# Layer 2 of a four-layer network on one core: B of the state scan broadcast one state ahead, banks shared anew, routing counts in two matmuls

## The chip, the cores and the metric

The kernel runs on one core of a Trainium2 chip. The metric is the device time of one execution in microseconds; lower is better. TensorE is called PE, VectorE DVE, ScalarE ACT, GpSimd POOL, and SyncE, which issues the DMAs, SP.

## The reference

Four layers follow each other, each an attention-like mixer, a gate computed by a feed-forward part, and `x = x + s * silu(ffn(xn))`. The tokens are 4096 rows of 128 features (the input of 16 x 256 tokens). The change touches layer 2 only. Its mixer is a selective state scan, its feed-forward part a choice of 2 of 16 expert banks for each token:

```
def step(h, inp):                       # 16 states n, 256 channels d
    dt_t, B_t, C_t, u_t = inp
    dA = jnp.exp(dt_t[..., None] * A)
    h = h * dA + (dt_t * u_t)[..., None] * B_t[:, None, :]
    y = jnp.einsum('bdn,bn->bd', h, C_t)
    return (h, y)
...
logits = jnp.einsum('bsd,de->bse', tensor, Wr) + br
probs = jax.nn.softmax(logits, axis=-1)
topv, topi = jax.lax.top_k(probs, NUM_SELECTED)          # 2 of 16
h = jax.nn.relu(jnp.einsum('bsd,edh->bseh', tensor, W1) + b1)
y = jnp.einsum('bseh,ehm->bsem', h, W2) + b2
```

## The kernel before

The stages run one after the other, each a block in which every engine has its own program, and semaphores order them. Two stages matter here.

**Routing** (`layer2_route`). The 4096 tokens go by in 8 chunks of 512 (TT = 4 groups of 128). One loop iteration i finishes layer 1's gate for chunk i (`gate_times`, `gate_finish`), normalises it (`ln_tensor` on PE, `ln_scalar` on ACT, `ln_vector` on DVE), and routes chunk i-1: PE makes the logits and turns the rows, DVE picks two banks of 16 with one-hot masks OA and OB (`select`), PE counts with triangular and all-one matrices how many tokens before each one chose the same bank (`counts`), DVE adds the running offset `r.base` and writes the places (`place`), and POOL scatters the rows with 8 indirect DMAs. DVE's order in an iteration is: copy of Y, product, `select(i-1)`, `gate_finish`, `place(i-1)`, `ln_vector`. PE's is: turn, logits, `ln_tensor`, `counts(i-1)`.

**Scan and experts** (`layer2_mix`). There are 8 chunks k of 512 tokens and 16 states n; g = 16k + n numbers the states. For each state the engines do this:

- PE broadcasts the rows B and C of the state over the partitions (`spread_states`, L1079 and L1081; two matmuls of 32 rows each, on different rows of the array), into banks 0 and 1. It waits first for DVE's drive and ACT's copy of the state before.
- ACT computes the decay DA (L1196, two exponentials) and copies C to CN (L1203).
- DVE multiplies DB = DU x B out of the bank (L1302, the drive) and runs the scan over 1024 columns (L1308), which needs the decay.
- POOL multiplies the state with C: CA for the near half (L1355), CB for the far half (L1362) and its sum YA (L1364). PE adds CA up in bank 5 (`add_near`, L1089, one state later).

Between the states lie two other lines of work. The head of chunk k+1 (`head(k + 1, n)`: norm, input projection, convolution, silus, dt, on steps 0 to 14) is spread over the steps of chunk k. And in steps 3 to 12 one tile of 128 routed rows a step goes through its expert, 10 tiles a chunk, 80 in all: PE turns the rows (`tile_rows`, L1105), ACT copies them to XT (L1209), PE multiplies with the first weights (`tile_hidden`, L1110), ACT applies relu (L1214, buffer H), PE multiplies with the second weights and adds the bias (`tile_out`, L1118 and L1119), ACT copies the result to YO (L1221) and SP stores it. At the end of a chunk DVE gates the sum (L1314 to L1320), PE projects it (`project`, L1096) and DVE adds the input (L1326).

PE's queue is in order, and its order in a step is written out by hand: B and C; `tile_rows(j)`; `tile_out(j-1)`; `tile_hidden(j)`; `project` in step 1; `add_near` of the state before; the head's matmuls. The expert's weights (578 KB a tile) and its rows (64 KB) have two buffers, and SP's program for them is:

```
for j in range(TILES):
    if j >= 2:
        sp.wait_ge(s.out_ready, j - 1)
    load_tile(j)
    if j >= 2:
        store_tile(j - 2)
```

`out_ready` is raised by the last matmul of `tile_out`, so that the load of tile j follows `tile_out(j-2)`, and `tile_rows(j)` waits for the load.

## Time and profile before

| | |
|---|---|
| three runs | 4656.27, 4648.75, 4588.19 us; median 4648.75 |
| profiled execution | 4658.04 us, span 4656.4 us |
| busy | PE 3423.9 us (74%), DVE 2642.8 (57%), ACT 1828.2 (39%), POOL 1538.3 (33%) |
| granted clock of PE, mean | 0.793 of 2.4 GHz |
| DMA | 111.46 MB in the whole, 63 GB/s in the scan stage |

Busy shares are means over stages with different limits; PE's busy time has modelled ends and is no measure of a full PE. The granted clock is at one of two levels at each moment, 1.0 (2.4 GHz) or 0.5 (1.2 GHz); a figure between is a mean over a stretch. The profile's "idle before" of an instruction tells what released its engine.

### The profile page before, as it was taken

To read this page: it belongs to the slowest core of one execution; us is meant where nothing else is said; L and a number is where in the kernel's file an instruction comes from. 1 tells how busy PE (TensorE), PEld (TensorE's weight loads), DVE (VectorE), ACT (ScalarE), POOL (GpSimd) and SP (SyncE) were. 2 spreads that over 40 slices of the span, in tenths; PEclk is the share of its full clock that TensorE was granted. 3 is DMA by queue.
4 is the path that set the end of the run, shared out by engine and by line. 5 is a ranking of instruction groups with operands and counts; after the bars stand their busy time and mean duration, and the time that the engine had idled before them with its cause. 6 is when DMAs were issued, how large, how long until landed. Compare 5 with 4: busy or idle time off the path is not lost. (4 is left out here: it accounts for less than half of the span.)

```text
span 4656.4 us, 50785 instructions
## 1 busy us (share of the span) xinstructions
PE 3423.9 (74%) x17802; PEld 1842.6 (40%) x17802; DVE 2642.8 (57%) x3696; ACT 1828.2 (39%) x3692; POOL 1538.3 (33%) x1231
## 2 busy tenths in 40 slices
PE   5888888883538788788757677676776857778587
PEld 3444444441424344344323334333343334343343
DVE  3444444442547777777655566555665656556565
ACT  3333333331214444444424434344343434434344
POOL 0000000003316665656644253332533424334242
PEclk8888888885557777777768879688797988959789
DMA  1000000002212222222100000000000000000000
GB/s 80 7 7 7 7 7 7 7 5 74 72 42 63 67 67 67 67 67 59 59 16 5 8 1 5 8 5 8 1 5 8 5 8 1 8 6 5 8 1 8
DMA packets 70704, 111.46 MB, mean 24 GB/s; under 512 B 8640, under 2 KB 46016, under 8 KB 69952
## 3 DMA queue, kind: packets, MB, share of 16 engines
q1 hardware_dynamic: 65088, 97.47, 6.5%
q0 software_dynamic: 5376, 11.02, 0.9%
q8 instruction: 123, 2.02, 0.2%
q14 instruction: 117, 0.96, 0.1%
HBM read 81.71 MB, written 26.74 MB: 23 GB/s over the span
## 5 line engine op out<-in xcount | busy, mean ns | idle before, releaser
L369 ACT ACTIVATE l_PT<-PB 128x512 f32<-128x512 f32 x512 | 277.9, 594 | 539.1 <-PE PB L280 539.1
L280 PE MATMUL PB<-l_QM,l_KP 32*128 32x256 f32 x2048 | 375.2, 497 | 131.6 <-DVE l_QM L418 75.9
L407 DVE TENSOR_REDUCE keep_MXP<-PB 128x4 f32<-128x1024 f32 x256 | 301.5, 1220 | 106.8 <-PE PB L253 106.8
L280 PEld LDWEIGHTS PB<-l_QM,l_KP 32*128 32x128 f32 x2048 | 241.3, 243 | 256.4 <-ACT l_PT L369 99.9
L1308 DVE TENSOR_TENSOR_SCAN l_ST<-l_DA,l_DB 128x1024 f32<-128x1024 f32 x128 | 313.7, 2451 | 42.0 <-ACT l_DA L1196 32.8
L1355 POOL TENSOR_TENSOR l_CA<-l_ST,l_CN 128x512 f32<-128x512 f32 x128 | 182.6, 1426 | 397.6 <-DVE l_ST L1308 346.0
L703 POOL MEMSET l_KV<- 128x4 f32 x8 | 0.8, 105 | 918.5 <-POOLq L109 918.5
L1515 POOL TENSOR_TENSOR l_PT<-l_PT,l_PEN 128x512 f32<-128x512 f32 x168 | 212.5, 1284 | 184.5 <-ACT l_PT L369 184.5
L1089 PE MATMUL PB<-l_CA,consts 128*128 128x512 f32 x256 | 199.2, 872 | 71.4 <-POOL l_CA L1355 71.4
L1779 POOL TENSOR_TENSOR l3f_SQ<-l3f_RW 128x512 f32<-128x512 f32 x128 | 146.8, 1147 | 302.4 <-ACT l3f_RW L1645 302.4
L1302 DVE TENSOR_TENSOR l_DB<-l_DU,PB 128x1024 f32<-128x1024 f32 x128 | 155.4, 1214 | 154.1 <-PE PB L1079 153.4
L1583 PE MATMUL PB<-l3f_QK 64*64 64x128 f32 x2048 | 159.3, 301 | 80.5 <-DVE l3f_QK L1719 80.5
L1788 POOL TENSOR_TENSOR l3f_PP<-l3f_PP,l3f_RS 128x512 f32<-128x512 f32 x128 | 133.1, 1040 | 251.2 <-DVE l3f_RS L1737 251.2
L1079 PE MATMUL PB<-l_BC,consts 32*128 32x512 f32 x256 | 180.9, 792 | 42.7 <-DVE l_DB L1302 22.0
L253 PE MATMUL PB<-l_KP,l_QP 32*128 32x256 f32 x2048 | 198.0, 514 | 15.6 <-issue 15.6
L1362 POOL TENSOR_TENSOR l_CB<-l_ST,l_CN 128x512 f32<-128x512 f32 x120 | 208.8, 1740 | 0.0
L1670 ACT ACTIVATE l3f_PP<-PB,l3f_MN 128x128 f32<-128x128 f32 x512 | 146.4, 368 | 157.6 <-DVE l3f_MN L1731 157.6
L294 PE MATMUL PB<-l_PT,keep_VT 128*32 128x256 f32 x2048 | 170.6, 490 | 35.2 <-POOL l_PT L1515 19.2
L418 DVE TENSOR_TENSOR l_QM<-l_QP,PB 128x256 f32<-128x256 f32 x128 | 53.9, 421 | 237.0 <-PE PB L262 233.5
L1364 POOL TENSOR_TENSOR l_YA<-l_YA,l_CB 128x512 f32<-128x512 f32 x120 | 184.2, 1535 | 9.4
L1401 POOL TENSOR_SCALAR l_T<-l_AJ,l_GI 128x256 f32<-128x256 f32 x16 | 18.4, 1147 | 504.0 <-DVE l_AJ L1491 504.0
L1081 PE MATMUL PB<-l_BC,consts 32*128 32x512 f32 x256 | 182.1, 797 | 0.0
(416 smaller groups left out, 7934.3 us busy)
## 6 DMA issues: line engine op xcount, KB each, us to landing
l_WB<-in_w2f_dram SPq DMA_DIRECT2D x80, 578.0 KB, 3.4
l_XR<-xs_mid SPq DMA_DIRECT2D x80, 64.0 KB, 3.5
ys_mid<-l_YO SPq DMA_DIRECT2D x80, 64.0 KB, 3.3
w3fs<-in_w3f_dram SPq DMA_DIRECT2D x1, 3125.0 KB, 16.6
keep_XI<-in_x_dram SPq DMA_DIRECT2D x9, 256.0 KB, 3.0
x_mid<-keep_X SPq DMA_DIRECT2D x9, 256.0 KB, 3.0
s_mid<-keep_S SPq DMA_DIRECT2D x9, 256.0 KB, 2.0
keep_SI<-s_mid SPq DMA_DIRECT2D x9, 256.0 KB, 2.6
```

The source lines that it names most:

```text
L253: last = nc.tensor.matmul(PB[:, r, qt * SEQ:(qt + 1) * SEQ], b.QP[rows, a, q0:q0 + 128], b.KP[rows, a, i, sq * SEQ:(sq + 1) * SEQ], start= ...
L280: last = nc.tensor.matmul(PB[:, 4 + u % STBANKS, kt * SEQ:(kt + 1) * SEQ], b.KP[rows, a, i, k0:k0 + 128], b.QM[rows, n % 2, :], start=True ...
L369: nc.scalar.activation(b.PT[:, u % PSLOTS].rearrange("p k q -> p (k q)"), PB[:, 4 + u % STBANKS, :], ACT.Exp).then_inc(s.exp_done, 1)
L407: nc.vector.tensor_reduce(dst[:, 2 * pair:2 * pair + 2, :, 16 + n % 2], PB[:, 2 * pair:2 * pair + 2, :].rearrange("p r (t k) -> p r t k", ...
L1079: nc.tensor.matmul(PB[:, 0, :], c.ident[0:32, n:n + 1].broadcast_to([32, 128]), b.BC[0:32, k % 2, :], start=True, stop=True).then_inc(s.b_ ...
L1081: nc.tensor.matmul(PB[:, 1, :], c.ident[32:64, 32 + n:33 + n].broadcast_to([32, 128]), b.BC[32:64, k % 2, :], start=True, stop=True).then_ ...
L1089: last = nc.tensor.matmul(PB[:, 5, :], c.ident, b.CA[:, g % 2, :], start=n == 0, stop=n == NS - 1)
L1308: nc.vector.tensor_tensor_scan(b.ST[:, g % 2].rearrange("p k t -> p (k t)"), b.DA[:, g % 2].rearrange("p k t -> p (k t)"), b.DB[:, g % 2]. ...
L1355: nc.gpsimd.tensor_tensor(b.CA[:, g % 2, :], b.ST[:, g % 2, 0, :], b.CN[:, g % 2, :], ALU.mult).then_inc(s.near_ready, 1)
L1362: nc.gpsimd.tensor_tensor(b.CB[:], b.ST[:, g % 2, 1, :], b.CN[:, g % 2, :], ALU.mult).then_inc(s.far_ready, 1)
L1364: last = nc.gpsimd.tensor_tensor(b.YA[:], b.YA[:], b.CB[:], ALU.add)
L1515: nc.gpsimd.tensor_tensor(pt, pt, b.PEN[:, 2 * sq:2 * sq + 2, :], ALU.mult).then_inc(s.weighed_pool, 1)
```

## The change

In the scan stage `spread_states` is split. `spread_drive(g)` broadcasts B into bank g % 2, one PE step ahead of its state, and waits for the drive of state g-2. `spread_output(g)` broadcasts C into bank 2 and waits for the copy of C of state g-1 alone. The turned rows of a tile and the tile's result now share bank 3 (the projection uses it too), and the hidden product moves to bank 4. PE's order in a step becomes: B of the next state, C of this one; `tile_rows(j)`; `project`; `add_near`; `tile_hidden(j)`; `tile_out(j-1)`; head. `tile_rows(j)` now waits for the result copy of tile j-2, `tile_hidden(j)` for the activations of tile j-1, and ACT's activations of tile j for `tile_out(j-1)`. ACT's own order, DVE's, POOL's and SP's stay.

In the routing stage the 14 count matmuls become two over all 64 columns, done ahead of `ln_tensor`; DVE forms the running offsets of the four groups in `r.base`, now five rows, with four chained adds, and `place` comes behind `ln_vector`.

```diff
-                    for t in range(TT):
-                        o = PB[:, 6, t * E2:(t + 1) * E2]
-                        nc.tensor.matmul(o, c.before, b.OC[:, t, :], start=True, stop=t == 0)
-                        for u in range(t):
-                            nc.tensor.matmul(o, c.ones, b.OC[:, u, :], start=False, stop=u == t - 1)
-                    for t in range(TT):
-                        last = nc.tensor.matmul(PB[:, 6, TT * E2:TT * E2 + E2], c.ones, b.OC[:, t, :], start=t == 0, stop=t == TT - 1)
-                    last.then_inc(s.count_ready, 1)
+                    each = b.OC[:].rearrange("p t e -> p (t e)")
+                    nc.tensor.matmul(PB[:, 6, 0:TT * E2], c.before, each, start=True, stop=True)
+                    nc.tensor.matmul(PB[:, 6, TT * E2:2 * TT * E2], c.ones, each, start=True, stop=True).then_inc(s.count_ready, 1)
...
                     if i:
                         logits(i - 1)
+                        counts(i - 1)
                     if i < CHUNKS:
                         pe.wait_ge(s.x_gated, i + 1)
                         ln_tensor(nc, pe, s, c, of(i).X, PB[:, 1:5], i)
-                    if i:
-                        counts(i - 1)
...
-                    link(nc.vector.tensor_tensor(b.WK[:], PB[:, 6, 0:TT * E2].rearrange("p (t e) -> p t e", e=E2),
-                                                 r.base[:].unsqueeze(1).broadcast_to([128, TT, E2]), ALU.add))
-                    nc.vector.tensor_tensor(r.base[:], r.base[:], PB[:, 6, TT * E2:TT * E2 + E2], ALU.add).then_inc(s.count_taken, 1)
+                    for t in range(TT):
+                        link(nc.vector.tensor_tensor(r.base[:, t + 1, :], r.base[:, t, :], PB[:, 6, (TT + t) * E2:(TT + t + 1) * E2], ALU.add))
+                    nc.vector.tensor_tensor(b.WK[:], PB[:, 6, 0:TT * E2].rearrange("p (t e) -> p t e", e=E2), r.base[:, 0:TT, :],
+                                            ALU.add).then_inc(s.count_taken, 1)
+                    dve.wait_ge(s.count_taken, k + 1)
+                    nc.vector.tensor_copy(r.base[:, 0, :], r.base[:, TT, :])
...
-                def spread_states(k, n):
-                    g = NS * k + n
+                def spread_drive(g):
+                    k, n = divmod(g, NS)
                     if n == 0:
                         pe.wait_ge(s.bc_copied, k + 1)
+                    if g >= 2:
+                        pe.wait_ge(s.drive_ready, g - 1)
+                    nc.tensor.matmul(PB[:, g % 2, :], c.ident[0:32, n:n + 1].broadcast_to([32, 128]), b.BC[0:32, k % 2, :],
+                                     start=True, stop=True).then_inc(s.b_ready, 1)
+
+                def spread_output(g):
+                    k, n = divmod(g, NS)
                     if g:
-                        pe.wait_ge(s.drive_ready, g)
                         pe.wait_ge(s.c_copied, g)
...
                 def tile_rows(j):
                     pe.wait_ge(tile_loaded[j % 2], 32 * (j // 2 + 1))
-                    if j:
-                        pe.wait_ge(s.rows_taken, j)
+                    if j >= 2:
+                        pe.wait_ge(s.out_taken, j - 1)
...
                 def tile_hidden(j):
                     pe.wait_ge(s.rows_taken, j + 1)
+                    if j:
+                        pe.wait_ge(s.hid_done, 4 * j)
...
-                        spread_states(k, n)
+                        g = NS * k + n
+                        if g == 0:
+                            spread_drive(0)
+                        if g + 1 < NS * CHUNKS:
+                            spread_drive(g + 1)
+                        spread_output(g)
                         j = SLOTS * k + n - FIRST
                         if FIRST <= n < FIRST + SLOTS:
                             tile_rows(j)
-                        if FIRST < n <= FIRST + SLOTS:
-                            tile_out(j - 1)
-                        if FIRST <= n < FIRST + SLOTS:
-                            tile_hidden(j)
...
                             add_near(k, n - 1)
+                        if FIRST <= n < FIRST + SLOTS:
+                            tile_hidden(j)
+                        if FIRST < n <= FIRST + SLOTS:
+                            tile_out(j - 1)
...
                 def tile_hidden(j):
                     act.wait_ge(s.hid_ready, j + 1)
+                    if j:
+                        act.wait_ge(s.out_ready, j)
```

## Rows read from the trace of the kernel before

**Rows 1.** Windows by stage: busy us (instructions) per engine, TensorE clock, DMA share, GB/s.

```profile
1390.00:2345.00 955.00, 753.66 (x2479) 375.92 (x2480) 681.89 (x442) 447.62 (x976) 582.57 (x376) 0.74 0.21 63
```

**Rows 2.** Windows of chunk 3's tile steps and end steps, and of chunk 4's tile steps.

```profile
1767.10:1844.30 77.20, 68.41 (x250) 38.32 (x251) 51.18 (x36) 38.80 (x92) 42.37 (x30) 0.76 0.31 91
1844.30:1889.90 45.60, 29.61 (x65) 10.26 (x65) 36.38 (x24) 18.82 (x34) 30.99 (x19) 0.70 0.06 17
...
1889.90:1964.10 74.20, 63.86 (x258) 36.65 (x259) 52.21 (x35) 39.02 (x92) 41.58 (x30) 0.84 0.29 94
```

**Rows 3.** Waits in the scan stage: us in total, times, longest.

```profile
DVE l_DB L1302 <- PE PB L1079: 153.4, 54, 8.0
...
PEld PB L1105 <- DMA l_XR<-xs_mid: 82.5, 42, 3.4
...
PE PB L1105 <- DMA l_XR<-xs_mid: 42.6, 29, 2.6
...
DVE l_ST L1308 <- ACT l_DA L1196: 32.8, 23, 2.4
```

**Rows 4.** Timeline of a plain tile step: start us, us, engine, line, operation.

```profile
1787.42 0.33 PE L1105 MATMUL PB<-consts,l_XR 128*128 128x128 f32 x1 [0.66 <-DMA l_XR<-xs_mid]
...
1788.58 0.48 PE L1119 MATMUL PB<-l_WB,consts 1*128 1x128 f32 x2
...
1788.99 1.16 PE L1110 MATMUL PB<-l_XT,l_WB 128*128 128x128 f32 x8
...
1790.34 0.33 SPq L1006 DMA_DIRECT2D l_WB<-in_w2f_dram  x1
...
1790.94 0.69 PE L1079 MATMUL PB<-l_BC,consts 32*128 32x512 f32 x1
...
1794.39 0.33 PE L1105 MATMUL PB<-consts,l_XR 128*128 128x128 f32 x1 [2.32 <-DMA l_XR<-xs_mid]
```

**Rows 5.** Timeline: hidden product and `add_near` at 1.2 GHz.

```profile
1716.48 2.08 PE L1110 MATMUL PB<-l_XT,l_WB 128*128 128x128 f32 x8
...
1718.35 1.92 PE L1089 MATMUL PB<-l_CA,consts 128*128 128x512 f32 x2
```

**Rows 6.** Timeline of chunk 3: state 3's product, states 8 and 10.

```profile
1770.74 1.27 POOL L1355 TENSOR_TENSOR l_CA<-l_ST,l_CN 128x512 f32<-128x512 f32 x1 [2.46 <-DVE l_ST L1308]
...
1806.40 2.08 PE L1110 MATMUL PB<-l_XT,l_WB 128*128 128x128 f32 x8 [1.41 <-ACT l_XT L1209]
...
1823.71 1.31 ACT L1196 ACTIVATE l_DA<-l_DL,keep_aneg 128x510 f32<-128x510 f32 x2
1823.79 1.22 DVE L1302 TENSOR_TENSOR l_DB<-l_DU,PB 128x1024 f32<-128x1024 f32 x1 [8.02 <-PE PB L1079]
...
1825.11 2.29 DVE L1308 TENSOR_TENSOR_SCAN l_ST<-l_DA,l_DB 128x1024 f32<-128x1024 f32 x1
```

**Rows 7.** Timeline of a chunk's end (chunks 2 and 3).

```profile
1746.24 1.26 POOL L1364 TENSOR_TENSOR l_YA<-l_YA,l_CB 128x512 f32<-128x512 f32 x1
...
1747.54 1.74 DVE L1317 SCALAR_TENSOR_TENSOR l_YG<-l_XC,w2s,l_YA 128x512 f32<-128x512 f32 x1 [1.67 <-POOL l_YA L1364]
...
1759.79 1.31 ACT L1196 ACTIVATE l_DA<-l_DL,keep_aneg 128x510 f32<-128x510 f32 x2
...
1761.19 2.29 DVE L1308 TENSOR_TENSOR_SCAN l_ST<-l_DA,l_DB 128x1024 f32<-128x1024 f32 x1 [0.39 <-ACT l_DA L1196]
```

**Rows 8.** Routing: timeline of one iteration; the last line is from the waits.

```profile
1230.09 0.22 DVE L874 TENSOR_TENSOR l2r_LO<-PB,w2s 128x64 f32<-128x64 f32 x1 [0.71 <-PE PB L813]
...
1236.37 2.07 PE L132 MATMUL PB<-l2r_X,consts 128*128 128x256 f32 x4 [5.43 <-DVEq L925]
...
1239.84 0.42 ACT L145 ACTIVATE keep_lnr<-keep_lnr 128x256 f32<-128x256 f32 x1
...
1245.97 0.23 DVE L896 TENSOR_TENSOR l2r_WK<-PB,r_base 128x64 f32<-128x64 f32 x1 [9.71 <-PE PB L831]
...
DVE l2r_WK L896 <- PE PB L831: 71.4, 8, 9.7
```

More of the change, by code:

```diff
@@ L913, in _ @@
                 nc.vector.memset(r.gate[:, :, TT * CHUNKS:], 0.0)
-                link(nc.vector.tensor_copy(r.base[:], c.expert))
+                link(nc.vector.tensor_copy(r.base[:, 0, :], c.expert))
                 for i in range(CHUNKS + 1):
@@ L925, in _ @@
                         dve.sem_inc(s.x_gated, 1)
-                    if i:
-                        place(i - 1)
                     if i < CHUNKS:
@@ L932, in _ @@
                         ln_vector(nc, dve, s, c, of(i).XN, PB[:, 1:5], link, i).then_inc(s.xn_ready, 1)
-                nc.vector.tensor_scalar(tails[:], r.base[:], 0.0, None, ALU.add).then_inc(s.tails_ready, 1)
+                    if i:
+                        place(i - 1)
+                nc.vector.tensor_scalar(tails[:], r.base[:, TT, :], 0.0, None, ALU.add).then_inc(s.tails_ready, 1)
                 full = c.full.unsqueeze(1).broadcast_to([128, E2, TOKENS // 128])
@@ L937, in _ @@
                 ends = b.EN[:].unsqueeze(1).broadcast_to([128, TILES, E2])
-                link(nc.vector.tensor_tensor(b.CT[:], r.base[:], c.expert, ALU.subtract))
+                link(nc.vector.tensor_tensor(b.CT[:], r.base[:, TT, :], c.expert, ALU.subtract))
                 link(nc.vector.tensor_tensor(b.NF[:], b.CT[:].unsqueeze(2).broadcast_to([128, E2, TOKENS // 128]), full, ALU.is_gt))
@@ L1093, in project @@
                     pe.wait_ge(s.y_gated, k + 1)
-                    pe.wait_ge(s.rows_taken, SLOTS * (k + 1))
+                    pe.wait_ge(s.out_taken, SLOTS * (k + 1))
                     for h in range(2):
-                        last = nc.tensor.matmul(PB[:, 2, :], w.out[:, h * 128:(h + 1) * 128], b.YG[:, h, :], start=h == 0, stop=h == 1)
+                        last = nc.tensor.matmul(PB[:, 3, :], w.out[:, h * 128:(h + 1) * 128], b.YG[:, h, :], start=h == 0, stop=h == 1)
                     last.then_inc(s.mamba_ready, 1)
@@ L1100, in tile_rows @@
                     pe.wait_ge(tile_loaded[j % 2], 32 * (j // 2 + 1))
-                    if j:
-                        pe.wait_ge(s.rows_taken, j)
+                    if j >= 2:
+                        pe.wait_ge(s.out_taken, j - 1)
                     if j % SLOTS == 0 and j:
                         pe.wait_ge(s.s_added, j // SLOTS)
-                    nc.tensor.transpose(PB[:, 2, 0:128], b.XR[:, j % 2, :], c.ident).then_inc(s.rows_ready, 1)
+                    nc.tensor.transpose(PB[:, 3, 0:128], b.XR[:, j % 2, :], c.ident).then_inc(s.rows_ready, 1)
                 def tile_hidden(j):
                     pe.wait_ge(s.rows_taken, j + 1)
+                    if j:
+                        pe.wait_ge(s.hid_done, 4 * j)
                     for i in range(4):
-                        last = nc.tensor.matmul(PB[:, 3, i * 128:(i + 1) * 128], b.WB[:, j % 2, i * 128:(i + 1) * 128], b.XT[:], start=True, stop=True)
+                        last = nc.tensor.matmul(PB[:, 4, i * 128:(i + 1) * 128], b.WB[:, j % 2, i * 128:(i + 1) * 128], b.XT[:], start=True, stop=True)
                     last.then_inc(s.hid_ready, 1)
@@ L1833, in network @@
         r2 = record(idx=whole("idx2", 2, tokens // 128 + TT), places=whole("places2", 2, TT), bank=whole("bank2", TILES),
-                    row=whole("row2", TILES), **buffers(nc, ctx, "r2", gate=[2, tokens // 128 + TT], base=[E2])._asdict())
+                    row=whole("row2", TILES), **buffers(nc, ctx, "r2", gate=[2, tokens // 128 + TT], base=[TT + 1, E2])._asdict())
         with ExitStack() as first:
```

22 lines of the change are left out of this document (9 added, 13 removed).

## Prediction

> **What bounds the kernel now.** I read the stage windows first, then the waits of the scan stage, then its timeline step by step. The profiled execution took 4658.04 us for a span of 4656.4, 1.6 us around it. The diff touches two stages: the routing, eight loop iterations between 1120 and 1315 us, and layer 2's scan, 955 us [rows 1]. The scan stage is 8 chunks of 16 states, about 7.4 us a state, and no engine fills it (DVE 682 us, POOL 583, PE 754 with modelled ends). So I asked in which order PE's queue releases the others. A chunk has two parts [rows 2]: the ten steps 3 to 12 with an expert tile (77.2 us here, 74.2 in chunk 4) and the six steps around the chunk's end (45.6 us).
>
> In the tile steps the reader is to see a loop that runs through the DMA queue. SP may load tile j only when `tile_out(j-2)` has ended. In one such step [rows 4] `tile_out` ends at 1788.58 + 0.48 = 1789.06; SP issues the weight load at 1790.34, 1.28 us later, and the transpose of the tile after next starts at 1794.39: 5.33 us for the round trip. Between the two PE does useful work: `tile_hidden` at 1788.99, `add_near`, the B/C pair at 1790.94. Then it still waits. 71 of the 80 transposes waited for a load, 82.5 + 42.6 = 125.1 us in all [rows 3]. Right behind the transpose comes `tile_out(j-1)` (1787.42 to 1789.06, 1.6 us), so a plain cycle now is 5.33 + 1.6 = 6.95 us.
>
> DVE waits 153.4 us for B in 54 places [rows 3], which is what the change is aimed at. But the scan behind it needs ACT's decay too: 32.8 us of waits beside, and in most places both arrive together. At 1823.79 DVE had waited 8.02 us for B, and the scan started at 1825.11, just behind the decay's end at 1823.71 + 1.31 = 1825.02 [rows 6]. An earlier B would have bought nothing.
>
> **The change, part by part.**
>
> *B one state ahead, two banks.* No instruction is added. B(g+1) is issued a PE step earlier and waits for the drive of g-1; C(g) alone waits for the copy of C(g-1). DVE's wait for B goes; next late is the decay. Going through the stage's timeline, I took for each wait the smaller of DVE's idle time and the decay's lead: steps 2, 8, 10, 12 and 13 give nothing, the rest about 3 us a chunk with a head and 20 in the last, 40 of 153.4 us. That is the upper bound. Most lies in tile steps, where the loop below decides, and the six steps at the chunk's end don't move either [rows 7]: POOL works without a gap until its add of 1746.24 lets DVE's 1747.54 start, then gate, `project`, `add_near`, the variance matmul, two ACT operations and the decay (1759.79) give the scan of 1761.19. None of these waits for B. I take 0; bound 0 to -40. C and B ran side by side on two row groups. In the tile steps both waits are long satisfied when PE comes to them and that stays; apart they would cost one more pair (1.1 us), hidden under the load wait. 0.
>
> *The tile order.* PE's old order in a step: B/C, transpose(j), `tile_out(j-1)`, `tile_hidden(j)`, `add_near`, head. New: B/C, transpose(j), `add_near`, `tile_hidden(j)`, `tile_out(j-1)`, head. SP's program is the same, so the load of the tile after next is still tied to the end of `tile_out`. `add_near` and `tile_hidden`, which lay inside the round trip, now lie between transpose and `tile_out`, outside it. Queued behind the wait for the load on PE are all of them, and DVE, ACT and POOL behind those. The B/C pair (1.1 us) and no more is left to fill the 5.33 us in a step without head work: this is where cover is lost. Price: `tile_hidden` to the end of `add_near`, as one sequence, 1788.99 to 1790.94 = 1.95 us at a granted 2.4 GHz [rows 4], and 1716.48 to 1718.35 + 1.92, 3.8 us, at 1.2 GHz [rows 5]. The tile window's granted clock is 0.76 [rows 2], half the time at each level, so 2.85 us. New plain cycle: 6.95 + 1.95 = 8.9 us at full clock.
> - Of the eight cycles of a chunk that depend on a load (tiles 2 to 9), five are plain: 40 x 2.85 = 114 us (78 to 152).
> - Three have other work in the chain. Step 5: the transpose no longer lets `tile_out` go first, and `add_near` then waits for POOL's product of the state just scanned, 1.27 us long [rows 6]: +1.5 us. Steps 8 to 9: ACT's table loads and silus, the decay and two copies come behind the hidden activations, and `tile_hidden` waited 1.41 us for XT already [rows 6]; now `tile_out` (1.6 us) stands behind that too, and `add_near` at most: +1 to +3, I take 2. The step with four head matmuls hides the round trip either way: +0.5. Together 4 x 8 = 32 us (12 to 50).
> - ACT's new wait: H(j) and all behind it on ACT (the head's activations, the next decay) wait for `tile_out(j-1)`. In the last tile step this sits in front of the table loads and the decay on which scan 13 waits; before, `tile_hidden` alone did. One `add_near` more, 1.1 to 2.1 us, 8 times: +14 (8 to 20).
>
> Sum of the scan stage: +160 us; the ends are +85 (full clock, some look-ahead kept) and +225 (half clock).
>
> *Banks.* Transpose and result share bank 3, B/C/tile use 0, 1, 2, 3, 4. The transpose waits for the result copy of tile j-2, which ACT does 0.3 us behind `tile_out(j-2)`, 5 us before the load lands: 0.
>
> *Routing.* One loop iteration is 24 us. DVE finishes the gate, PE starts the norm at 1236.37, and DVE sits 9.71 us until the counts are there, at 1245.97; eight such waits are 71.4 us [rows 8]. PE does the layer norm first and then 14 small matmuls. Now two matmuls are done before the norm, in the time in which DVE gates. What is late next: the norm's reciprocal root, first half at 1239.84 + 0.42 = 1240.26, 4.0 us behind the gate's end instead of 9.7: -5.7. `place` moves behind `ln_vector`, so it covers PE's logits, on which DVE waited 0.7: -0.7. Four chained 16-column adds and a copy for one add: +0.9, estimated at the 0.2 us a link that such small operations stand apart. Net -5.5 us, 7 iterations: -38. At the end POOL's queue holds: the scatters of chunk 6 last 10 us and those of 7 stand behind, so the last iteration gives 1 us at most. Moved past SP's and POOL's queues is only `place`'s release of the scatters, 8 x 1.26 us in an 18 us iteration: covered. I take -37 (-30 to -42).
>
> **Total:** +160 - 37 = +123 us, so 4658 + 123 = 4781 for a profiled run. The median shown is 9 us under that run: 4648.75 + 123 = 4772, written as 4770.
>
> **The clock.** In the window of the plain cycles PE's granted clock is 0.76; in the six steps at the chunk's end, with longer gaps between matmuls, 0.70 [rows 2]. With 8.9 us cycles PE waits over 3 us in each. The Trainium skill ("TensorE: Matmul & The Clock Gate", section "HAM oscillation — how this bites in real kernels") says that a loop which waits for a DMA between short bursts of matmuls falls back to half clock in every round. By the row above the price of half clock in all cycles is 3.8 us instead of 2.85, and the lengthened rows the same way. This is rival 2; the rule alone would give its time.
>
> **Rivals.**
> 1. *The same loop, but the clock stays full in the tile steps* and the three special cycles absorb: +85 - 37 = +48, 4697 us. For: nearly half of the windows are at 2.4 GHz now. Against: the gaps get longer.
> 2. *Half clock throughout the tile steps:* +225 - 37 = +188, 4837 us. For: row and rule above. Against: chunk 4 ran 0.84 at cycles of 6.7 us.
> 3. *Faster: the look-ahead decides, and the longer cycle doesn't bind.* DVE's 40 us are saved and routing gives 37: 4572 us. It needs the load to be there when PE comes to the transpose, that is a round trip under the 1.1 us pair plus the head; from 71 waits of 80 I hold it for unlikely. It decides if PE's wait for the load in a plain step stays under about 2 us.
> 4. *The change doesn't do what it says:* C's wait on the copy of C(g-1) stalls the pair in each step and B is no earlier where it matters. Then the gain in the scan is nil, as in my forecast, and the time is the forecast's.
>
> **How the numbers follow.** Forecast with rival 4: 0.58; rival 1: 0.20; rival 2: 0.12; rival 3: 0.07; something that cancels to about zero: 0.03. Two per cent of 4648.75 is 93 us, about what a measurement of this kernel can tell from no change; the limit above is 4742. Of the forecast's own spread some 0.10 lies under it. So slower 0.60, within 2% 0.33, faster 0.07. The range for 8 in 10: from 4695 (rival 1) to 4845 (rival 2).
>
> **What would show it.** In the changed profile: transposes start about 5.3 us behind the end of `tile_out` of two tiles before, as now, but PE's waits for the load rise from 125 us to 300 or more; tile steps take 9 to 12 us each, none 6.7; the tile part of a chunk is 90 to 97 us, the six other steps 44 to 46. DVE's wait for B is nearly gone, its scan waits for the decay instead, and DVE's busy time is unchanged. Routing: iterations of 18.4 us, the wait for the counts gone, 4 us of wait for the root in its place. The prediction is wrong if the transposes find the load landed, if the end part shrinks by more than 2 us a chunk, or if the granted clock in the tile part moves outside 0.6 to 0.85.

## The result, and the profile after

The changed kernel took 4850.26 us in the median of four runs (4829.98 to 4865.49), the kernel before 4641.16 (four runs, 4588.19 to 4656.27): a ratio of 1.047, with a 95% interval of 1.038 to 1.056. It is slower, as forecast, but at +209 us instead of +123, and its time lies 5 us above the upper end of the range. All medians and ranges here and below hold every execution, while the ratios leave out the few of the kernel before that ran in the chip's slower state. The profiled execution took 4865.49 us for a span of 4863.8, 207.4 more than the span of before.

The windows by stage show where these lie. First those of before, of whose three stages only the middle one stands in [rows 1], there from 1390 to 2345; here the bounds are the issue of the scan's first input (1347) and the end of its last scan (2335), so that the stage is 988 us and not the 955 of the prediction. The columns are those of [rows 1], the granted clock is the third figure from the right.

```profile
0.00:1347.00 1347.00, 964.92 (x5194) 564.88 (x5194) 563.17 (x1144) 419.81 (x795) 111.85 (x123) 0.77 0.07 26
1347.00:2335.00 988.00, 773.95 (x2506) 381.39 (x2506) 695.53 (x460) 463.00 (x993) 576.43 (x375) 0.74 0.21 63
2335.00:4656.00 2321.00, 1685.00 (x10103) 896.38 (x10102) 1384.09 (x2093) 945.34 (x1904) 850.06 (x734) 0.83 0.02 6
```

The same three stages of the changed kernel:

```profile
0.00:1304.00 1304.00, 924.14 (x4994) 525.22 (x5002) 568.78 (x1176) 419.81 (x795) 108.26 (x123) 0.79 0.08 27
1304.00:2478.00 1174.00, 792.79 (x2504) 415.68 (x2504) 680.02 (x460) 457.23 (x993) 576.34 (x374) 0.72 0.17 53
2478.00:4864.00 2386.00, 1735.97 (x10016) 935.87 (x10104) 1382.29 (x2092) 944.50 (x1904) 850.85 (x735) 0.79 0.02 6
```

The scan stage is 186 us longer, with DVE, ACT and POOL no busier than before. The first line holds layers 0 and 1 and the routing, 43 us less. The last line holds layer 3, which the diff doesn't touch: 65 us more, DVE, ACT and POOL busy within 2 us of before, PE at a granted clock of 0.79 instead of 0.83. So the +207 is two effects of the change (+186 and about -39, below) and two things that it did not edit: 65 us in layer 3 and -4 in layers 0 and 1.

**The tile loop** is the prediction's loop. These are chunk 3's tile steps and its end steps, against [rows 2]:

```profile
1791.60:1887.00 95.40, 67.07 (x249) 42.45 (x248) 51.07 (x36) 37.24 (x90) 41.64 (x30) 0.73 0.22 67
1887.00:1936.90 49.90, 34.34 (x69) 11.70 (x68) 35.70 (x25) 19.74 (x34) 31.96 (x19) 0.63 0.10 29
```

The waits of the scan stage (us in total, times, longest), against [rows 3]:

```profile
DVE l_ST L1316 <- issue: 331.4, 46, 12.4
...
PEld PB L1106 <- DMA l_XR<-xs_mid: 272.2, 64, 6.1
PE PB L1106 <- DMA l_XR<-xs_mid: 219.3, 64, 5.3
...
DVE l_ST L1316 <- ACT l_DA L1202: 53.0, 9, 6.4
```

The drive's wait for B has no line any more (153.4 us before). The scan waits in its place. Its wait is put down to "issue", but it is the decay: all 60 scans of the trace that waited began 0.09 to 0.44 us behind the decay's end. The two rows of PE and PEld tell of the same transposes, first of the weight load and then of the matmul of each, so they must not be added. Taken by the matmul rows alone, PE's waits for the load went from 42.6 us in 29 places to 219.3 in 64, and these 64 are all the transposes whose load is tied to the loop.

A plain tile cycle, against [rows 4]. To read it, take the end of `tile_out` (the second line of L1120, 1821.92 + 0.27 = 1822.19), the weight load that SP issues (1823.47), and then the next transpose (L1106, 1827.49), which waits for a load. That load, issued at 1823.47, is the one that this end released.

```profile
1817.21 0.34 PE L1106 MATMUL PB<-consts,l_XR 128*128 128x128 f32 x1 [2.34 <-DMA l_XR<-xs_mid]
1817.38 1.02 PE L1090 MATMUL PB<-l_CA,consts 128*128 128x512 f32 x2
...
1818.24 1.68 PE L1113 MATMUL PB<-l_XT,l_WB 128*128 128x128 f32 x8
1819.71 1.92 PE L1119 MATMUL PB<-l_WB,l_H 128*128 128x128 f32 x8
...
1821.92 0.27 PE L1120 MATMUL PB<-l_WB,consts 1*128 1x128 f32 x1
...
1823.47 0.33 SPq L1003 DMA_DIRECT2D l_WB<-in_w2f_dram  x1
...
1827.49 0.48 PE L1106 MATMUL PB<-consts,l_XR 128*128 128x128 f32 x1 [4.43 <-DMA l_XR<-xs_mid]
1827.76 1.92 PE L1090 MATMUL PB<-l_CA,consts 128*128 128x512 f32 x2
...
1829.46 1.92 PE L1113 MATMUL PB<-l_XT,l_WB 128*128 128x128 f32 x8
...
1831.17 1.52 PE L1119 MATMUL PB<-l_WB,l_H 128*128 128x128 f32 x8
...
1832.84 0.27 PE L1120 MATMUL PB<-l_WB,consts 1*128 1x128 f32 x1
```

The round trip is 1822.19 to 1827.49, 5.30 us, as it was (5.33). What changed is the stretch from the transpose to the end of `tile_out`: 1817.21 to 1822.19 = 4.98 us, and 1827.49 to 1833.11 = 5.6 in the next cycle, where it had been 1.6. In the second of them, behind a wait of 4.43 us, the transpose (0.48 us), `add_near` (1.92) and `tile_hidden` (1.92) run at 1.2 GHz, where full clock gives 0.33, 1.02 and 1.16. Over `tile_out` behind them the granted clock is 0.75 in the mean: part of it runs at 2.4 GHz again.

The step with ACT's silus shows what the scan waits for:

```profile
1834.47 1.28 ACT L1170 ACT_TABLE_LOAD   x1
...
1837.90 1.28 ACT L1174 ACT_TABLE_LOAD   x1
...
1839.19 1.33 ACT L1202 ACTIVATE l_DA<-l_DL,keep_aneg 128x510 f32<-128x510 f32 x2
...
1840.61 2.29 DVE L1316 TENSOR_TENSOR_SCAN l_ST<-l_DA,l_DB 128x1024 f32<-128x1024 f32 x1 [12.37 <-issue]
```

DVE had its drive ready 12.37 us before the scan, and the scan still started at the decay's end, 1839.19 + 1.33 = 1840.52. The table loads before it stood behind the activations of the tile, and these behind `tile_out`.

The chunk's end, against [rows 7]:

```profile
1915.96 1.26 POOL L1372 TENSOR_TENSOR l_YA<-l_YA,l_CB 128x512 f32<-128x512 f32 x1
1917.49 1.49 DVE L1325 SCALAR_TENSOR_TENSOR l_YG<-l_XC,w2s,l_YA 128x512 f32<-128x512 f32 x1
...
1929.58 1.31 ACT L1202 ACTIVATE l_DA<-l_DL,keep_aneg 128x510 f32<-128x510 f32 x2
1930.98 2.29 DVE L1316 TENSOR_TENSOR_SCAN l_ST<-l_DA,l_DB 128x1024 f32<-128x1024 f32 x1 [3.82 <-issue]
```

From POOL's add to the scan it is 15.02 us, before 14.95. The windows from drive to drive make the end part look 4 us longer (49.9 against 45.6), because the drive of state 13 now runs ahead of its scan. Counted from scan to scan (scan 13 of a chunk to scan 2 of the next) the seven chunk ends take 35.5 us in the mean, before 35.8; the other part of these seven chunks, scan 2 to scan 13, takes 107.4 against 84.8.

One routing iteration, against [rows 8]:

```profile
1149.72 0.69 DVE L915 COPY keep_Y<-PB 128x512 f32<-128x512 f32 x1
...
1155.44 0.63 PE L827 MATMUL PB<-l2r_OC,consts 128*128 128x64 f32 x2
...
1161.66 0.43 DVE L153 TENSOR_TENSOR keep_lnt<-keep_lnr 128x256 f32<-128x256 f32 x1 [4.13 <-ACT keep_lnr L145]
...
1168.42 0.69 DVE L915 COPY keep_Y<-PB 128x512 f32<-128x512 f32 x1
```

The iteration takes 18.7 us (24 before), and the wait of 4.1 us for the root stands where 9.7 us for the counts stood. From the first copy of Y to the scan's first input the routing took 225.2 us before (1121.85 to 1347.03) and 186.6 after (1117.45 to 1304.07): -38.6.

### The profile page after: what moved, and what is told of

Same layout as the page of the kernel before. It is cut to its first block and busy times, and to the rows that moved or that the text cites. A ratio compares the mean times of both kernels' runs of the same rounds, so it can differ in the third digit from the quotient of the medians.

```text
span 4863.8 us, 50294 instructions
## 1 busy us (share of the span) xinstructions
PE 3452.9 (71%) x17514; PEld 1876.8 (39%) x17610; DVE 2631.1 (54%) x3728; ACT 1821.5 (37%) x3692; POOL 1535.5 (32%) x1231
## 5 line engine op out<-in xcount | busy, mean ns | idle before, releaser
L1316 DVE TENSOR_TENSOR_SCAN l_ST<-l_DA,l_DB 128x1024 f32<-128x1024 f32 x128 | 305.4, 2386 | 391.0 <-issue 331.4
L280 PE MATMUL PB<-l_QM,l_KP 32*128 32x256 f32 x2048 | 390.2, 514 | 131.6 <-DVE l_QM L418 76.0
L1363 POOL TENSOR_TENSOR l_CA<-l_ST,l_CN 128x512 f32<-128x512 f32 x128 | 197.2, 1541 | 583.6 <-DVE l_ST L1316 581.6
L1090 PE MATMUL PB<-l_CA,consts 128*128 128x512 f32 x256 | 226.2, 982 | 103.3 <-POOL l_CA L1363 103.3
L1591 PE MATMUL PB<-l3f_QK 64*64 64x128 f32 x2048 | 171.1, 317 | 88.0 <-DVE l3f_QK L1727 80.5
L253 PE MATMUL PB<-l_KP,l_QP 32*128 32x256 f32 x2048 | 209.8, 541 | 15.6 <-issue 15.6
L294 PE MATMUL PB<-l_PT,keep_VT 128*32 128x256 f32 x2048 | 182.4, 518 | 34.1 <-POOL l_PT L1523 19.2
L1370 POOL TENSOR_TENSOR l_CB<-l_ST,l_CN 128x512 f32<-128x512 f32 x120 | 192.7, 1606 | 0.0
L1106 PE MATMUL PB<-consts,l_XR 128*128 128x128 f32 x80 | 34.4, 430 | 219.3 <-DMA l_XR<-xs_mid 219.3
L1082 PE MATMUL PB<-l_BC,consts 32*128 32x512 f32 x256 | 175.2, 769 | 19.6 <-ACT l_CN L1209 19.6
L1591 PEld LDWEIGHTS PB<-l3f_QK 64*64 64x64 f32 x2048 | 136.4, 159 | 115.5 <-issue 112.3
```

Of the source, the lines that this page charges most:

```text
L253: last = nc.tensor.matmul(PB[:, r, qt * SEQ:(qt + 1) * SEQ], b.QP[rows, a, q0:q0 + 128], b.KP[rows, a, i, sq * SEQ:(sq + 1) * SEQ], start= ...
L280: last = nc.tensor.matmul(PB[:, 4 + u % STBANKS, kt * SEQ:(kt + 1) * SEQ], b.KP[rows, a, i, k0:k0 + 128], b.QM[rows, n % 2, :], start=True ...
L294: last = nc.tensor.matmul(PB[32 * r:32 * r + 32, 7, 0:SEQ], VT[:, 2 * sq + kt, 8 * a + 2 * r + i, :], b.PT[:, (NR * (2 * j + i) + r) % PSL ...
L1090: last = nc.tensor.matmul(PB[:, 5, :], c.ident, b.CA[:, g % 2, :], start=n == 0, stop=n == NS - 1)
L1316: nc.vector.tensor_tensor_scan(b.ST[:, g % 2].rearrange("p k t -> p (k t)"), b.DA[:, g % 2].rearrange("p k t -> p (k t)"), b.DB[:, g % 2]. ...
L1363: nc.gpsimd.tensor_tensor(b.CA[:, g % 2, :], b.ST[:, g % 2, 0, :], b.CN[:, g % 2, :], ALU.mult).then_inc(s.near_ready, 1)
```

## The experiments

Eleven runs: ten other kernels and the changed one again, in three sets, each set timed in rounds beside the kernel before on one chip; the first set (route_only, old_order, no_lookahead, three_buffers) ran on one chip and the other two on another. The medians of before in the three sets were 4637.17 us (19 runs), 4621.88 (7) and 4637.73 (13). "Scan stage" is from the issue of its first input to the end of its last scan; before it was 988.2 us. That is one trace; route_only, whose scan stage is the same code, gives a second value for the old stage, 959.2. Losses of the stage below are counted from 988.2 and would be 29 us larger from the other.

| kernel | scan stage us | granted clock in it | layer 3 us | clock in it | median us | ratio, 95% interval |
|---|---|---|---|---|---|---|
| before, the profiled execution | 988.2 | 0.738 | 2321.1 | 0.827 | | |
| changed, first trace | 1173.7 | 0.717 | 2386.1 | 0.794 | 4850.26 | 1.047 (1.038 to 1.056) |
| route_only | 959.2 | 0.760 | 2350.4 | 0.809 | 4611.04 | 0.994 (0.990 to 0.998) |
| old_order | 1108.8 | 0.691 | 2341.9 | 0.815 | 4718.54 | 1.017 (1.011 to 1.022) |
| no_lookahead | 1173.9 | 0.717 | 2309.9 | 0.828 | 4809.62 | 1.040 (1.035 to 1.045) |
| three_buffers | 992.4 | 0.751 | 2334.3 | 0.818 | 4638.61 | 1.002 (0.999 to 1.005) |
| after_again | 1173.8 | 0.715 | 2311.2 | 0.828 | 4807.37 | 1.039 (1.033 to 1.045) |
| order_alone | 1176.9 | 0.716 | 2330.2 | 0.818 | 4835.46 | 1.046 (1.039 to 1.052) |
| shared_alone | 1104.5 | 0.701 | 2314.0 | 0.825 | 4769.63 | 1.031 (1.025 to 1.037) |
| best_three | 931.2 | 0.779 | 2304.2 | 0.830 | 4549.95 | 0.985 (0.979 to 0.992) |
| route_outfirst | 941.2 | 0.787 | 2310.9 | 0.829 | 4568.41 | 0.986 (0.977 to 0.994) |
| outfirst_three | 945.2 | 0.773 | 2337.2 | 0.817 | 4589.05 | 0.993 (0.989 to 0.998) |
| near_ahead | 1099.4 | 0.675 | 2329.1 | 0.818 | 4761.57 | 1.026 (1.018 to 1.035) |

For the orders I read off the timeline, for each of the eight steps whose load is tied to the loop, the trip (end of `tile_out(j-2)` to the transpose of tile j) and the stretch (that transpose to the end of `tile_out(j-1)`). The two together are one cycle. A trip near 5.3 us is the load's round trip; a longer one holds work that takes longer than the load. Medians over the chunks, in us:

| step | 5 | 6 | 7 | 8 | 9 | 10 | 11 | 12 | sum |
|---|---|---|---|---|---|---|---|---|---|
| before, trip | 7.17 | 5.37 | 5.26 | 5.65 | 7.13 | 7.54 | 5.34 | 5.56 | 49.0 |
| before, stretch | 1.64 | 1.64 | 1.87 | 2.62 | 2.27 | 1.64 | 1.64 | 1.64 | 15.0 |
| changed, trip | 5.52 | 5.30 | 5.28 | 5.40 | 5.35 | 5.42 | 5.28 | 5.47 | 43.0 |
| changed, stretch | 4.88 | 4.97 | 5.04 | 7.04 | 5.65 | 3.78 | 5.89 | 5.34 | 42.6 |
| order_alone, stretch | 5.03 | 4.98 | 5.17 | 7.22 | 5.69 | 3.84 | 5.84 | 5.32 | 43.1 |
| shared_alone, stretch | 2.59 | 2.33 | 2.48 | 7.17 | 2.69 | 3.75 | 3.82 | 4.42 | 29.3 |
| near_ahead, stretch | 3.93 | 3.20 | 4.16 | 4.61 | 4.61 | 2.49 | 4.36 | 4.38 | 31.7 |

**The theory.** The time of a tile step is the load's round trip plus whatever PE does between the transpose and the end of `tile_out`; the new order put two pieces of work there. The rivals: the new banks or ACT's new wait cost it, or the look-ahead; and for layer 3, that the change itself slows it.

**route_only.** The routing part alone; `layer2_mix` is the old one.

> The kernel before with the routing part of the change alone. Both theories: the routing stage is 43 us shorter (Y-copy period 18.7 us instead of 24), the scan stage stays at 985 us as before. They differ on layer 3, whose code nobody touched and which took 2287 us before and 2351 after. Theory (its length goes by the granted clock it happens to meet): anywhere in 2280 to 2360 us, with granted clock and length moving together. Rival (the larger offset buffer, which moves the addresses of what lies behind it, slows layer 3): 2340 us or more. Time 4600 us by the theory with layer 3 as before, 4665 by the rival.

The ratio is 0.994, a gain of 26 us by the medians, with an interval of 9 to 48 us; the routing takes 186.3 us (1103.70 to 1289.97) as in the changed kernel, 38.9 less than before. The scan stage, whose code is the old one to the letter, took 959.2 us instead of 988.2, at a clock of 0.760 instead of 0.738, and layer 3 took 2350 at 0.809:

```profile
1290.00:2249.00 959.00, 743.23 (x2504) 365.46 (x2504) 699.27 (x460) 463.85 (x993) 594.18 (x374) 0.76 0.21 65
2249.00:4600.00 2351.00, 1717.56 (x10104) 918.31 (x10104) 1383.12 (x2093) 944.81 (x1904) 850.34 (x735) 0.81 0.02 6
```

So the old scan stage moves by 29 us from one execution to another. The expectation of a scan stage at 985 was wrong, and the one on layer 3 leaned to the rival until the next kernels: the larger offset buffer is in no_lookahead, after_again and best_three too, whose layer 3 took 2304 to 2311. The addresses are not the cause.

**no_lookahead.** B in its own step again, all else as changed.

```diff
-                        if g == 0:
-                            spread_drive(0)
-                        if g + 1 < NS * CHUNKS:
-                            spread_drive(g + 1)
+                        spread_drive(g)
...
-                    if g >= 2:
-                        pe.wait_ge(s.drive_ready, g - 1)
+                    if g:
+                        pe.wait_ge(s.drive_ready, g)
```

> The changed kernel with B broadcast in its own state's step again, behind the drive of the state before, as C's neighbour. Theory (the look-ahead buys nothing, since the decay comes later anyway): scan stage 1165 to 1190 us, time 4840 to 4880. Rival 1 (it bought the 20 to 40 us that the order then took away): scan stage 1195 to 1215. Rival 2 (B ahead of C costs, being issued in front of the load wait): scan stage under 1150.

1173.9 us, the changed kernel's 1173.7 within 0.2. The median, 4809.62, lies 30 us under the 4840 to 4880 that I expected; I had carried over the 2386 us that layer 3 took in the first trace of the changed kernel, and here it took 2310. In the old order the look-ahead buys nothing either: old_order, which has it, took 1108.8 us, and shared_alone, which has not, 1104.5. The drive's wait for B is back, larger than ever, and costs nothing, for the decay is as late:

```profile
DVE l_DB L1307 <- PE PB L1075: 292.1, 69, 11.0
...
DVE l_ST L1313 <- ACT l_DA L1199: 96.9, 44, 5.4
```

**old_order.** PE's tile order put back, look-ahead and banks kept; since rows and result share bank 3, `tile_out(j-1)` waits for `rows_taken(j)`.

```diff
                         if FIRST <= n < FIRST + SLOTS:
                             tile_rows(j)
+                        if FIRST < n <= FIRST + SLOTS:
+                            tile_out(j - 1)
+                        if FIRST <= n < FIRST + SLOTS:
+                            tile_hidden(j)
...
-                        if FIRST <= n < FIRST + SLOTS:
-                            tile_hidden(j)
-                        if FIRST < n <= FIRST + SLOTS:
-                            tile_out(j - 1)
```

> The changed kernel with PE's tile order put back: rows, out of the tile before, hidden, add_near. Look-ahead, banks and ACT's order stay as changed; since rows and result share a bank, out waits for the copy of the rows. Theory (the round trip of the load plus what stands outside it sets a tile step): hidden and add_near are inside the round trip again, plain tile steps 7.3 to 7.8 us, the scan stage 985 to 1015 us, the time 4600 to 4660. Rival (the new banks, C's own wait or ACT's wait for tile_out cost it): the scan stage stays above 1100 us.

1109 us, and 4718.54 for the whole. The theory fell, and the rival's mark (above 1100) was met. The order gives back 65 us, not 160 to 190: with the new banks something costs about 120 us in the old order too, and the next two kernels take it apart.

**order_alone.** The kernel before with the new order only (the same moves the other way, with waits of `tile_hidden(j)` for `hid_done` of tile j-1 and of ACT's activations for `out_ready`), old banks. The two waits belong to the order: the activations write the buffer H that `tile_out(j-1)` now still has to read.

> The kernel before with PE's new tile order alone: rows, add_near, hidden, out of the tile before, in the old banks, B and C together in their own step, routing as before. Theory (hidden and add_near outside the load's round trip are the whole loss): scan stage 1150 to 1190 us, time 4800 to 4860. Rival (the shared bank carries a part of it, as the old order with the shared bank, at 1109 us, suggests): scan stage 1060 to 1120.

1176.9 us against the changed kernel's 1173.7: the order with its two waits, without the new banks and the look-ahead, gives the whole loss, and its stretches are those of the changed kernel step by step (43.1 against 42.6 us a chunk).

**shared_alone.** The kernel before with rows and result in bank 2:

```diff
-                    if j:
-                        pe.wait_ge(s.rows_taken, j)
+                    if j >= 2:
+                        pe.wait_ge(s.out_taken, j - 1)
...
-                    if j:
-                        pe.wait_ge(s.out_taken, j)
+                    if (j + 1) % SLOTS:
+                        pe.wait_ge(s.rows_taken, j + 2)
...
-                    nc.scalar.activation(b.YO[:, j % 2, :], PB[:, 4, 0:128], ACT.Copy).then_inc(s.out_taken, 1)
+                    nc.scalar.activation(b.YO[:, j % 2, :], PB[:, 2, 0:128], ACT.Copy).then_inc(s.out_taken, 1)
```

> The kernel before with the turned rows and the result of a tile in one bank, and nothing else: tile_out(j-1), still right behind the rows of tile j, now waits for ACT's copy of them. Theory (that copy stands behind the decay and the copy of C on ACT, and so behind POOL's far product, and this wait lies outside the round trip): scan stage 1080 to 1125 us, as with look-ahead (1109). Rival (the look-ahead in the old order cost it): 985 to 1015 us.

1104.5 us, as old_order (1108.8). The silu step shows the wait:

```profile
1859.53 0.33 PE L1105 MATMUL PB<-consts,l_XR 128*128 128x128 f32 x1 [0.83 <-DMA l_XR<-xs_mid]
...
1862.07 1.33 ACT L1196 ACTIVATE l_DA<-l_DL,keep_aneg 128x510 f32<-128x510 f32 x2
1863.31 0.57 ACT L1203 ACTIVATE l_CN<-PB 128x512 f32<-128x512 f32 x1
...
1863.78 0.27 ACT L1209 ACTIVATE l_XT<-PB 128x128 f32<-128x128 f32 x1
...
1864.19 2.04 PE L1118 MATMUL PB<-l_WB,l_H 128*128 128x128 f32 x8 [4.33 <-ACT l_XT L1209]
```

`tile_out` waits 4.33 us for a copy of rows that stands behind table load, decay and the copy of C on ACT; before, it followed the transpose at once. In the changed kernel the shared bank costs nothing beside the order (order_alone and the changed kernel are alike), since there `tile_hidden(j)`, which needs the same copy, stands ahead of `tile_out(j-1)` anyway. Both edits put `tile_out(j-1)` behind ACT's queue; either alone costs 116 to 189 us, and together they cost no more than the order.

**near_ahead.** The kernel before with `add_near` alone moved between the transpose and `tile_out`.

> The kernel before with add_near alone moved: rows, add_near, out of the tile before, hidden. It prices one of the two pieces that the change put between rows and out. Theory (each piece between rows and out lengthens the tile cycle by its own time, 1.1 to 2.0 us, and the step after POOL's table work by the wait for POOL's product): plain steps 8.1 to 8.9 us, scan stage 1050 to 1090 us, about half of the way to the whole new order at 1177. Rival (hidden, with its wait for ACT's copy of the rows behind decay and C copy, is the costly one): under 1040.

1099.4 us, a little over the theory's 1050 to 1090; of the plain cycles step 6 takes 8.7 us in the mean and steps 7, 11 and 12 take 9.6 to 9.8, where the theory had 8.1 to 8.9. `tile_out` begins behind an `add_near` that runs at half clock after the wait for the load, and then runs at half clock itself:

```profile
1826.92 0.47 PE L1105 MATMUL PB<-consts,l_XR 128*128 128x128 f32 x1 [1.40 <-DMA l_XR<-xs_mid]
...
1827.18 1.92 PE L1089 MATMUL PB<-l_CA,consts 128*128 128x512 f32 x2
...
1828.89 1.92 PE L1118 MATMUL PB<-l_WB,l_H 128*128 128x128 f32 x8
...
1830.74 0.79 PE L1119 MATMUL PB<-l_WB,consts 1*128 1x128 f32 x2
```

The stretch is 1826.92 to 1831.53, 4.6 us, where the piece itself at full clock would make it 1.64 + 1.02 = 2.7. Of the order's 189 us, `add_near` alone brings 111.

**three_buffers.** The changed kernel with the load of tile j tied to `tile_out(j-3)`. Of the edit, SP's program (weights and rows have three buffers in the rest of it):

```diff
-                    if j >= 2:
-                        sp.wait_ge(s.out_ready, j - 1)
+                    if j >= 3:
+                        sp.wait_ge(s.out_ready, j - 2)
                     load_tile(j)
-                    if j >= 2:
-                        store_tile(j - 2)
+                    if j >= 3:
+                        store_tile(j - 3)
```

> The changed kernel with three buffers for the expert's weights and rows: the load of tile j follows tile_out(j-3), and the store of tile j-3 follows it. Three other buffers lie on ones unused in this stage, to make room. Theory (the load's round trip sets the tile step): PE's waits for the load fall from 491 us to under 60, plain tile steps to 7 us or less, the scan stage to 940 to 1000 us, time 4560 to 4650. Rival (the chain through ACT, hidden, relu, out, copy, or the granted clock sets it): the waits for the load go, others take their place, the scan stage stays above 1080 us.

992.4 us, at the upper end of the theory's range. The matmul row of PE's waits for the load is gone (219.3 us to none, the weight-load row 272.2 to 1.6), and 181 of the 186 us come back with nothing else undone. That does not mean that the whole loss ran through the round trip, for a third buffer gains in the old order too: best_three below, with the old order and banks, took 931.2 us, 57 less than before. With three buffers the new stage (with the look-ahead and the new banks, too) is still 61 us behind the old one. So about two thirds of the loss, some 124 us, needs the round trip, and a third does not. What holds the new order then is not settled by a run. By PE's matmul rows `add_near` waits 124.7 us for POOL's product, and `tile_hidden`, with `tile_out` behind it, 61.6 us for ACT's copy of the rows.

**after_again.** The changed kernel once more.

> The changed kernel once more, unaltered, for a second trace. Theory (layer 3, whose code is the same, takes what the granted clock of that run gives): scan stage again 1165 to 1180 us, since its loop is the same, layer 3 somewhere in 2310 to 2390 with the clock that belongs to it, and the time 4790 to 4870. Rival (the change itself puts layer 3 into a worse phase): layer 3 again at 2380 to 2390 us with a clock of 0.79 or 0.80, time 4850 or more.

```profile
1324.00:2498.00 1174.00, 791.83 (x2504) 416.58 (x2504) 678.16 (x460) 457.07 (x993) 576.38 (x371) 0.72 0.17 53
2498.00:4809.00 2311.00, 1675.38 (x10104) 897.02 (x10104) 1381.43 (x2092) 944.87 (x1904) 850.45 (x735) 0.83 0.02 6
```

The scan stage is the same to 0.1 us, the routing to 0.1 (186.56), and layer 3 took 2311 us at 0.828 instead of 2386 at 0.794. The 65 us are no effect of the change.

**best_three, route_outfirst, outfirst_three.** What the runs pointed to: the new routing with the old scan, its round trip taken off the path in one of two ways. best_three has the three buffers of above. route_outfirst keeps two and moves `tile_out(j-1)` the other way:

```diff
-                        if FIRST <= n < FIRST + SLOTS:
-                            tile_rows(j)
                         if FIRST < n <= FIRST + SLOTS:
                             tile_out(j - 1)
+                        if FIRST <= n < FIRST + SLOTS:
+                            tile_rows(j)
                         if FIRST <= n < FIRST + SLOTS:
                             tile_hidden(j)
```

> The routing part of the change on the old scan stage, with three buffers for the expert's weights and rows, in the old order and the old banks. Theory (PE's 125 us of waits for the load in the stage before go; next late is the chain of decay, scan and POOL's three products, 7 us or less a plain step): scan stage 920 to 965 us, time 4540 to 4600. Rival (as in the changed kernel with three buffers, other chains take over at once): scan stage 975 to 995, time 4600 to 4640.

> The routing part of the change on the old scan stage and its banks, with tile_out(j-1) moved the other way: ahead of the rows of tile j, on PE alone. Two buffers, as before. Theory (the load of tile j+1 now starts a whole cycle before its rows are wanted, so the round trip of 5.3 us runs beside the cycle and its waits go): scan stage 925 to 955 us, about what three buffers gave (931), time 4540 to 4580. Rival (rows, hidden and the activations come 1.3 us later in each step, and that chain now counts): 960 to 1000 us.

> The same with three buffers. Theory: the load is off the path in either, so a third buffer adds nothing: scan stage within 15 us of the run with two. Rival (with out first the load still binds in the short steps): 20 us or more below it.

All three came out by their theories: 931, 941 and 945 us, and medians of 4549.95, 4568.41 and 4589.05. In route_outfirst the load of a tile is issued one cycle earlier, and its transpose finds it there:

```profile
1747.23 0.33 PE L1102 MATMUL PB<-consts,l_XR 128*128 128x128 f32 x1
...
1748.59 0.33 SPq L1003 DMA_DIRECT2D l_WB<-in_w2f_dram  x1
...
1754.61 1.16 PE L1115 MATMUL PB<-l_WB,l_H 128*128 128x128 f32 x8
1755.70 0.48 PE L1116 MATMUL PB<-l_WB,consts 1*128 1x128 f32 x2
1756.11 0.33 PE L1102 MATMUL PB<-consts,l_XR 128*128 128x128 f32 x1
```

Both best_three (4549.95) and route_outfirst (4568.41) beat the kernel before, by 1.5 and 1.4%, less than 2% but with intervals that leave out no change, and the changed one by some 5%. Against the 959 us of route_only, the same scan code, the gain of the stage is 28 and 18 us instead of 57 and 47. The third buffer adds nothing to the order with `tile_out` first.

## Why the prediction was right or wrong

**What bounds the kernel: right in the loop, with one count misread.** Transposes start 5.3 to 5.5 us behind the end of `tile_out` of two tiles before, the eight tied cycles take 9.2 to 12.4 us, and a chunk's tile part takes 91.7 to 96.8 ("90 to 97"). order_alone shows the order as the cause, three_buffers the round trip as the way in which two thirds of it cost. The prediction's "71 of the 80 transposes waited, 125.1 us" added the weight-load row (42) to the matmul row (29) of the same transposes. 42 of the 80 waited, and PE's matmuls lost 42.6 us. The sign "from 125 to 300 or more" carries the same double count; added up in that way it came to 491, and by the matmul rows it is 42.6 to 219.3. No term of the sum used it; the chance of rival 3 did, and 42 waits of 80 would have made a weaker case against it.

**B one state ahead, 0: right**, and measured: 1173.7 with, 1173.9 without. The scan starts with the decay. The end steps did not move: 35.5 us from scan to scan against 35.8. My own mark for them ("44 to 46" in windows from drive to drive) was badly chosen, since the look-ahead moves the drive.

**Banks, 0: right in the new order, for a reason I did not give.** order_alone with the old banks took 1176.9, the changed kernel 1173.7. I weighed only the transpose's wait for the result copy. The other wait, of `tile_out` for the rows' copy, costs 116 us in the old order (shared_alone) and is hidden in the new one.

**The tile order, +160: the mechanism was right, the term was mis-sized, in three places that partly cancel.** Measured +185.5, which the trace divides as follows.
- The eight tied cycles: I had 146. By the table (medians) they grew by 21.6 us a chunk, 173 in all, and by the means 169. Step 5 gave +1.6 (I had 1.5), steps 6, 7, 11 and 12 +3.3, +3.2, +4.2 and +3.6 (2.85 each), steps 8 and 9 +5.8 together (2.85 + 2), step 10 nothing (0.5). The step that failed is "2.85 for a plain cycle", the two moved pieces at the mean of both clocks. They ran mostly at 1.2 GHz: in these four steps 30 of 32 transposes took 0.46 us or more, and from the transpose to the start of `tile_out` it took 3.4 to 3.7 us (before 0.17). `tile_out` behind them took 1.47 us in steps 6 and 7, as before, and 1.7 to 2.2 in steps 12 and 11.
- The steps ahead of the first tied cycle: I had nothing. From scan 2 to the end of the chunk's first `tile_out` it took 15.4 us in the mean, before 11.4: +32 in eight chunks. This `tile_out` too now stands behind `add_near` and `tile_hidden`, and the wait for POOL's product that I put into step 5 stands here in step 4, up to 2.1 us.
- The end of the tile part: I had +14 on top of cycle 12. From the end of the chunk's ninth `tile_out` to scan 13 it now takes 6.0 us instead of 7.7: -14. Counted from the last tile's transpose to scan 13 it is 11.3 against 9.6, +1.7 a chunk, where the prediction's terms make 2.85 + 1.75. The last `tile_hidden` stood ahead of scan 13 in the old order as well, and I charged it a second time.

The chunk ends and the rest of the stage took 2 us less. That the stage came within 26 us of +160 is thus in part luck: 32 us left out, 28 us too much at the end, 23 too little in the cycles by the means.

The measured 3.6 us of a plain cycle is close to my price at half clock, 3.8; this is what rival 2 said of the plain steps. The Trainium skill's section "HAM oscillation — how this bites in real kernels" ("TensorE: Matmul & The Clock Gate") has it that a loop which waits for a DMA between short bursts starts each burst at half clock. In the plain steps the trace agrees, by the 30 transposes of 32. Rival 2 was not right for the whole tile part: the mean clock there is 0.71 to 0.78, inside my 0.6 to 0.85. It is 0.54 to 0.66 in the stretches of seven of the eight tied steps and 0.96 in step 10's, and 0.75 to 1.0 in the trips between them.

**Routing, -37: right.** Measured -38.6 in each of the two traces of the changed kernel; iterations of 18.7 us where I had 18.4, wait for the root 4.1 (4.0).

**The sum: the two stages give +147 in both traces (185.5 - 38.6) against my +123.** That alone would have stood inside the range. What carried the time out of it is the other step that failed, the assumption under the sum that all else stays ("so 4658 + 123 = 4781 for a profiled run"). It does not. Layer 3, untouched, took 2304 to 2386 us in the thirteen traces of the table, longer as its granted clock fell (0.830 to 0.794), and the first trace of the changed kernel had the longest. And the old scan stage, with which I compared, is itself 959 or 988 us by the clock it meets, while the changed one gave 1173.7 and 1173.8. The range had terms for what I priced and none for this. By the second four runs of the changed kernel, with a median of 4807.37 us, the same forecast would have held its range, so on which side of the upper end it came out was chance. Where the first four runs of the changed kernel got their low clock (0.774 to 0.783, while the second four had 0.786 to 0.789 and 4800 to 4820 us) is not settled; only one of the four has a trace.

**Rivals.** 1 and 3 fell: no plain step kept the full clock, and in none of the 64 tied steps was the load there. Rival 4's stall of C did not occur: PE's matmul for C waits 19.6 us for the copy of C, the same as the pair did before. That B earlier buys nothing was the forecast's own term.

## What to carry to other kernels

In a loop that is closed by a transfer, find the instruction that releases it, and count what stands between the one that waits for the data and that release. All of it is added to the trip. Work inside the trip is free as long as it fits (here into 5.3 us). To shorten such a loop, put the release first (here `tile_out` ahead of the next transpose) or give the transfer one buffer more; either was worth about as much here, and doing both no more. An order that puts more in front of the release can cost beside the loop too: with three buffers 61 us of the loss were left. An operand that is only one of two needed (B, where the decay comes as late) brings nothing when it comes early, however large its wait is in the profile. When a wait is shown once for the weight load and once for the matmul of one instruction pair, take one of the two. And a bank that two steps share can tie one of them to another engine's whole queue.

## What the runs showed of the hardware

- The time of this kernel goes with PE's granted clock, which differs from run to run with nothing changed; why it differs is not shown. In 39 runs of the kernel before, shown beside the experiments, the mean clock lay between 0.780 and 0.804 and the time between 4583.68 us (at 0.804) and 4707.56 (at 0.781); a straight line through them gives 46 us for 0.01 of clock, with a correlation of -0.98. In layer 3 with its fixed code: 2304 us at 0.830, 2334 at 0.818, 2350 at 0.809, 2386 at 0.794.
- A loop with long waits can be steadier than a full one: the changed scan stage repeated within 0.2 us in three kernels' traces (1173.7, 1173.8 and, without look-ahead, 1173.9), the old one moved by 29 us.
- Behind a wait for a load PE mostly starts at 1.2 GHz, and the more so the longer the wait. In the first trace of the changed kernel 35 of 36 transposes that had waited over 3.5 us took 0.46 us or more instead of 0.33, 18 of 20 that had waited 2 to 3.5 us, and none of 7 that had waited less than 1 us. In the trace of before it was 1 of 29, though eleven of these had waited 2.2 to 2.6 us: the length of the wait alone does not decide it.
